# Masks of a 16-head attention: one half written to PSUM by ScalarE and one half added by TensorE products, changed to all written by ScalarE

## What is computed

```
score = jnp.einsum('bhqd,bhkd->bhqk', qh, kh) / jnp.sqrt(jnp.float32(DEPTH))
score = score + mask * jnp.float32(-1000000000.0)
attn = jax.nn.softmax(score, axis=-1)
out = jnp.einsum('bhqk,bhkd->bhqd', attn, vh)
```

```
logits = (logits + bias[None, None]) / jnp.sqrt(jnp.asarray(D, dt))
logits = jnp.where(mask, logits, jnp.finfo(dt).min)
```

## Time and profile before

| | us |
|---|---|
| median of 3 runs | 1736.21 |
| lowest and highest of them | 1733.26, 1736.88 |
| the profiled execution | 1738.16 |
| its span, from its first to its last instruction | 1736.3 |
| PE busy | 1259.2 |
| DVE busy | 1009.3 |
| ACT busy | 885.4 |
| POOL busy | 499.7 |

### The profile page before, as it was taken

The page is one execution under the profiler, slowest core; times in us unless marked ns, Lnnn a source line. Parts: engine busy times, 40 slices in busy tenths (PEclk is TensorE's granted clock), DMA queues, the critical chain, the costliest instruction groups (busy, mean ns, idle before and its releaser), DMA issues. The chain is left out here.

```text
span 1736.3 us, 21579 instructions
## 1 busy us (share of the span) xinstructions
PE 1259.2 (73%) x7168; PEld 628.1 (36%) x7168; DVE 1009.3 (58%) x2042; ACT 885.4 (51%) x1822; POOL 499.7 (29%) x583
## 2 busy tenths in 40 slices
PE   6998645266666749866537996973985979888896
PEld 2575421022222215522213553431433434543462
DVE  2573456999999536413833644442734748736852
ACT  2673234599999546743013772231652564743653
POOL 0362002388888531100302210000200213422440
PEclk9999866589999978978865997975887799989998
DMA  3000000000000034011023400014411500000000
GB/s 136 2 2 2 19 8 0 1 0 0 0 1 0 0 112 90 2 43 37 0 79 66 81 2 35 0 31 107 92 51 37 110 13 39 1 1 1 0 2 13
DMA packets 43486, 52.73 MB, mean 30 GB/s; under 512 B 2800, under 2 KB 39792, under 8 KB 41968
## 3 DMA queue, kind: packets, MB, share of 16 engines
q1 hardware_dynamic: 43376, 51.35, 11.4%
HBM read 36.66 MB, written 14.68 MB: 30 GB/s over the span
## 5 line engine op out<-in xcount | busy, mean ns | idle before, releaser
L1341 POOL TENSOR_TENSOR L_attn_z<-L_attn_state,L_attn_r 128x1024 f32<-128x1024 f32 x64 | 150.8, 2358 | 40.0 <-DVE L_attn_state L1327 33.5
L1327 DVE TENSOR_TENSOR_SCAN L_attn_state<-bank,L_attn_w 128x512 f32<-128x512 f32 x128 | 149.0, 1205 | 0.0
L1238 PE MATMUL bank<-L_attn_z,const 128*128 128x512 f32 x256 | 138.1, 667 | 1.4 <-POOL L_attn_z L1345 1.4
L791 DVE CUSTOM_DVE_ANT_0 L_xattn_core_logits<-bank,L_xattn_mask 128x256 f32<-128x256 f32 x256 | 98.6, 422 | 53.9 <-PE bank L574 41.4
L146 PE MATMUL bank<-x,weights 128*128 128x512 f32 (+1 forms) x108 | 60.0, 711 | 59.6 <-PEq L181 26.1
L1222 PE MATMUL bank<-L_attn_rows,L_attn_select 128*128 128x512 bf16 x96 | 36.9, 442 | 86.1 <-ACT L_attn_C L1290 43.2
L1278 ACT ACTIVATE L_attn_r<-L_attn_after_dt,L_attn_half_guard,L_attn_A 128x512 f32<-128x512 f32 x128 | 96.5, 802 | 0.0
L1268 ACT ACTIVATE bank<-L_attn_dt,L_attn_A 128x510 f32<-128x510 f32 x128 | 86.5, 676 | 13.3 <-DVE L_attn_state L1327 13.3
L703 ACT ACTIVATE L_xattn_core_probs<-bank 128x512 f32<-128x512 f32 x132 | 71.5, 596 | 36.9 <-PE bank L617 25.5
L574 PE MATMUL bank<-L_xattn_core_rows 48*128 48x256 bf16 x384 | 64.6, 312 | 32.2 <-DMA L_xattn_core_rows<-L_xattn_core_slots 18.0
L1345 POOL TENSOR_TENSOR L_attn_z<-L_attn_z,L_attn_C 128x1024 f32<-128x1024 f32 x32 | 75.7, 2367 | 23.7 <-ACT L_attn_C L1290 23.6
(11 more groups left out here) (466 smaller groups left out, 3029.9 us busy)
## 6 DMA issues: line engine op xcount, KB each, us to landing
L_xattn_core_rows<-L_xattn_core_slots SPq DMA_DIRECT2D x24, 384.0 KB, 5.8
weights<-in_pack_L_ffn SPq DMA_DIRECT2D x2, 2118.5 KB, 7.9
L_xattn_core_slots<-L_xattn_core_k_parts SPq DMA_DIRECT2D x24, 128.0 KB, 2.0
L_attn_core_rows<-L_attn_core_slots SPq DMA_DIRECT2D x8, 384.0 KB, 5.5
weights<-in_pack_L_ffn SPq DMA_DIRECT2D x1, 2824.0 KB, 9.4
weights<-in_pack_L_attn SPq DMA_DIRECT2D x1, 2304.0 KB, 8.5
L_xattn_core_slots<-L_xattn_core_q_parts SPq DMA_DIRECT2D x12, 192.0 KB, 2.2
weights<-in_pack_L_xattn SPq DMA_DIRECT2D x1, 1539.5 KB, 6.2
```

The lines of the kernel that those rows point to most:

```text
L791: last = nc.vector.tensor_tensor_reduce(logits[:, c], scores_bank[side][:, c * S:(c + 1) * S], mask[:, 2 * b + c, :], 1.0, MASKED, ALU.add ...
L1238: last = nc.tensor.matmul(y_bank[2 * c + half][:], ident, z[:, g % NS, c], start=False, stop=False, skip_group_check=True)
L1327: nc.vector.tensor_tensor_scan(state[:, g % NS, c, ::step], a_bank[c][:, ::step], w[:, g % 2, c, ::step], 0.0, ALU.mult, ALU.add).then_inc ...
L1341: nc.gpsimd.tensor_tensor(z[:, g % NS], state[:, g % NS], r[:, g % NS], ALU.mult).then_inc(z_done, 1)
```

## The change

The whole mask of both sides is now written by ACT, and everything that served the other way is gone:

- `preload(p)` writes two banks (two instructions) where it wrote one, and `shifted(p)` waits for both. No product of a masked stage starts a bank anew.
- the 6 products L617 of each step are gone, and `shifted_done` rises after each side's last L607 product, as it did in the stages without a mask.
- the making of `mask_parts` is gone: L680 and L683 on ACT, L744 and L748 on POOL, with their semaphores, their buffer and the two waits for `mask_split`.
- all four banks are marked as written at the start (4 products at L555 where there were 2).

```diff
@@ block.tensor
-                for at in (1, 3):
+                for at in range(4):
                     last = nc.tensor.matmul(shifted_bank[at][:], K.w("ident"), K.x[:, 0:HALF], start=True, stop=True)
...
                 if masked:
-                    pe.wait_ge(preloaded, p + 1)
+                    pe.wait_ge(preloaded, 2 * p + 2)
...
-                                         start=(not masked or c == 0) and not preloads(side), stop=False,
-                                         skip_group_check=True)
+                                         start=not masked, stop=False, skip_group_check=True)
                     for side in range(2):
-                        done = not masked or preloads(side)
                         last = nc.tensor.matmul(banks[side][:, c * S:(c + 1) * S], K.minus_rows[side_rows(side), t],
-                                                shifts[side_rows(side), n % 2, :], start=False, stop=done,
+                                                shifts[side_rows(side), n % 2, :], start=False, stop=True,
                                                 skip_group_check=True)
-                        if c == 1 and done and not masked:
+                        if c == 1:
                             last.then_inc(shifted_done, 1)
-                if masked:
-                    if p % SPB == 0:
-                        pe.wait_ge(mask_split, b + 1)
-                    for c in range(2):
-                        for part in range(3):
-                            last = nc.tensor.matmul(banks[0][:, c * S:(c + 1) * S], K.ident_bf,
-                                                    mask_parts[:, part, b, c * S:(c + 1) * S], start=False,
-                                                    stop=(part == 2), skip_group_check=True)
-                    last.then_inc(shifted_done, 2)
@@ block.scalar
             def preload(p):
                 n, t = divmod(p, 2)
-                nc.scalar.activation(shifted_bank[2 * t + 1][:], flat_mask(n // NG8), ACT.Copy).then_inc(preloaded, 1)
+                for side in range(2):
+                    nc.scalar.activation(shifted_bank[2 * t + side][:], flat_mask(n // NG8), ACT.Copy
+                                         ).then_inc(preloaded, 1)
 
             if masked:
-                for b in range(B):
-                    nc.scalar.activation(mask_parts[:, 0, b], flat_mask(b), ACT.Copy).then_inc(mask_rounded, 1)
-                for b in range(B):
-                    act.wait_ge(mask_less, b + 1)
-                    nc.scalar.activation(mask_parts[:, 1, b], mask_rest[:, b], ACT.Copy).then_inc(mask_rounded2, 1)
                 act.wait_ge(written, 1)
...
-                if masked and n == 1 and at == 0:
-                    act.wait_ge(mask_split, B)
@@ block.gpsimd
-            if masked:
-                for b in range(B):
-                    pool.wait_ge(mask_rounded, b + 1)
-                    nc.gpsimd.tensor_tensor(mask_rest[:, b], flat_mask(b), mask_parts[:, 0, b], ALU.subtract
-                                            ).then_inc(mask_less, 1)
-                for b in range(B):
-                    pool.wait_ge(mask_rounded2, b + 1)
-                    nc.gpsimd.tensor_tensor(mask_parts[:, 2, b], mask_rest[:, b], mask_parts[:, 1, b], ALU.subtract
-                                            ).then_inc(mask_split, 1)
```

## The result

| | before | after |
|---|---|---|
| median of 18 runs each, us | 1735.58 | 1738.63 |
| lowest and highest, us | 1733.26, 1736.88 | 1736.69, 1742.27 |
| profiled execution, and its span, us | 1738.16, 1736.3 | 1739.85, 1737.9 |

The ratio after to before is 1.0021, with a 95% interval of 1.0013 to 1.0028: 3 us slower by the medians, at the edge of what this kernel's measurement can tell from no change.

A forecast was written before the change was run, and what follows sets the result against it. PE's mask products bound the masked loops, then ACT would: +2.2 loop, -1.4 start, +0.5 allowance make +1.3 a stage, +2.6 for both, so 1736.2 + 2.6 = 1738.8 us; range 1733 to 1750.

The forecast's parts named there:

- the likeliest case: Whole kernel: measured within 0.2% of no change, 1732.7 to 1739.7 us, chance 0.53; slower 0.40, faster 0.07.
- The turn-over: Masked loops: ACT, with 12.8 us free, gets 15.0 and becomes the bound; loop 74.5 us, 2.2 longer.
- The second preload: ACT in the masked loop: one more 128x512 preload adds 0.50 us in each of 30 steps, 15.0 us.
- The start: Start of each masked loop: without the first six mask products the first exponential comes about 1.4 us earlier.
- The prelude: Before the masked loop: removing the sixteen ACT and POOL instructions that made mask_parts gains nothing, hidden behind DMA and scores.
- The allowance: Masked loops, near step 12 and at the start: ACT still waits 0.5 us a stage, bounds 0 and 2.
- rival 1: PE's clock falls in the masked loops: a third of steps lose 0.5 us, 10 us for both, 1749; chance 0.20.
- One sign of being wrong: Masked loops: the forecast is wrong if ACT's idle before exponentials remains over 5 us a stage.
- Rival 2: ACT's second preload costs 0.60, or engine waits add 0.1 a step: +6 for both stages, 1745; chance 0.15.
- Rival 3: Norm behind the attention: products L207 may get full clock, -3 us, with further gains 1732.5; chance 0.07.
- Rival 4: Masked loops: scores or values still hold PE, loop stays 72.3 us, -1.4 a stage at best, 1733.5; chance 0.03.

The follow-up runs named there:

- prelude_back: The changed kernel with the making of the unused mask_parts put back (8 instructions on ACT, 8 on POOL); 1740.26 us, ratio 1.0040.
- changed_again: The changed kernel run once more with the same code, for a second trace; 1738.85 us, ratio 1.0019.
- pe_only: The kernel before without the six mask products L617 a step, side 0 left unmasked, one preload a step as before; 1717.26 us, ratio 0.9905.
- act_only: The kernel before with a second ACT preload a step, PE waiting for both and the mask products L617 kept; 1743.6 us, ratio 1.0054.
- fill3: The changed kernel with three more PE products of zeros (128x256) in every step; 1742.67 us, ratio 1.0042.

## Why the prediction was right

**The time.** Forecast 1738.8, measured 1738.63; +2.6 against +3.0 by medians. That the two times agree within 0.2 us is luck in part, since the median of before was taken as 1736.21 and came out as 1735.58. A ratio within 0.2% was the likeliest case and slower the next, and 1.0021 lies on that bound.

**The turn-over** held. The sum of ACT's list was 74.5 us; the shortest loops of the changed kernel are 74.65 and 74.92 (prelude_back 74.75), and 74.3 to 74.4 without their disturbed steps. Steps of 2.15 and 2.41 us were forecast, 2.16 and 2.42 measured. The second preload was taken as 0.50; a pair now takes 1.06 until the next instruction (681.69 to 682.75) against 0.54 for one, so it is 0.52. An estimate of 0.52 is what the Trainium skill's figure gave (page "ScalarE: Activation LUTs", section "What ACT_TABLE_LOAD costs", 186 ns + 0.833 ns an element less 93 ns), and here it was nearer than the row of a pair alone. The 0.6 us that this adds was given back: two exponentials take 1.10 us until the preload and not 1.11 (0.3 in thirty steps), the logarithm and exponential of the sums 0.72 a time and not 0.82, and four exponentials in a row at the end 2.04 us and not 2.16.

**One reading was too simple.** The steady step of 2.18 is not the mean step of before. Over eight steps with `gathered` and the reciprocals the kernel before needs 19.52 us and the next eight 19.29, the changed one 19.51 to 19.53 where no step is disturbed: there they are nearly equal. The 2.3 us that the loop of changed_again lost are in the first ten steps (+1.2) and the last five (+0.6), where PE before had no `values` yet or no more scores to make, with 0.5 in between, most of it one disturbed step (3.19 us where its like take 2.88). The sum over the whole loop, on which the forecast went, contains this; the comparison of 2.28 with 2.18 does not.

**The start** was forecast 1.4 earlier and was 1.4 to 1.9 in four stages, 1.7 on average. The moment forecast for it, near 658.0, was missed because this execution reached the stage 1.5 us later. **The prelude** gave nothing back in the traces, as said: the first scores are under the DMA and the first exponential comes 17 us after ACT's preloads.

**The allowance** of 0.5 us a stage was half right in its reason and too small. It stood for `values` that ACT would wait for, near step 12 and at the start, with a block of `values` at the lower clock laid bare once as the upper bound. At the start this came true: the sixth exponential waits at a clock of 0.50, behind such a block, in three of the four loops of the changed kernel:

```profile
668.06 1.94 PE L615 MATMUL bank<-L_xattn_core_probs,v_heads 128*32 128x256 f32 x16
...
671.42 1.08 ACT L680 ACTIVATE L_xattn_core_rest<-bank 128x512 f32<-128x512 f32 x2 [0.32 <-PE bank L598]
```

That step came 0.4 to 0.6 us late. Later on, at full clock, no such wait is there (changed_again at 1010 to 1020 us); there ACT waited with the falls of the clock, which the forecast had only in rival 1. Together both cost 0.8, 3.1, 0.3 and 0.6 us in the four loops, 1.2 on average and over the bound of 2 in one. What this adds to the forecast, 0.7 a stage, is half made up by the start (0.3 more gained) and the loop without disturbances (0.1 less). So the mechanism was right and the sum is right within 0.3 us a stage, in part because the errors of its terms ran against each other.

One sign of being wrong did show in one place: ACT's idle before exponentials was to stay under 5 us a stage. It was 4.2 us in the first stage, and 5.8 in the second, of which 3.6 are before the first exponential and the rest is mostly the falls of the clock.

**Rival 1** happened as a mechanism and not as a price. The forecast listed a PEclk of 1.00 through most of the loop as its sign, and 0.79 to 0.85 was measured; by that sign it was wrong. The clock was 0.50 until 672.95 us where it had risen at 661.35 before, and it fell again three times. But a step was taken to decide above 2.28 us, with 2.36 for one at the lower clock. In the first steps, which have no `values`, exponentials were 2.16 and 2.42 apart at clock 0.50 too, with ACT busy 9.84 of 10: PE's list just fits. Only steps with `values` in double or with the sums came out longer. So the price of a third of the steps at 0.5 each, 10 us for both stages, was in fact 0.9 us (changed_again) to 3.9 (after) by the late steps of the traces, the sixth exponential included. The small idles between groups of products that come with it are the 0.40, 0.48 and 0.68 us shown above, after which the clock fell at 686.8 us; the Trainium skill (page "TensorE: Matmul & The Clock Gate", section "A second HAM failure mode: psum-queue depth-cycling") says that such idles can bring the clock up and down. The trace agrees with that in its order of events, though no run changed the idles by themselves, and not with the weight the rule would have had: the loop paid for few of its falls.

**Rival 2** is out: pairs take 1.12 us, under its sign of 1.15, and preloads 591 ns. **Rival 3**: the norm's four products L207 took 2.69 and 2.53 us in the first trace, 3.75 and 3.27 in the second, against 3.75 and 2.0. Together that is 0.5 less and 1.3 more for the same code, so the change doesn't decide it; the durations go with the clock that was granted at that moment. The rows, two of the first trace and one of the second:

```profile
740.13 2.69 PE L207 MATMUL bank<-L_xattn_outT,weights 128*128 128x512 f32 x4 [2.56 <-PEq L478]
...
1043.76 2.53 PE L207 MATMUL bank<-L_xattn_outT,weights 128*128 128x512 f32 x4 [2.56 <-PEq L478]
```

```profile
739.12 3.75 PE L207 MATMUL bank<-L_xattn_outT,weights 128*128 128x512 f32 x4 [2.56 <-PEq L478]
```

**Rival 4** is out: PE was released, as pe_only's loops of 64.8 and 65.2 us show.

## What to carry to other kernels

Where two engines work in turn, add up the whole list of the one that is to receive the work, over the whole loop, before anything else: here 12.8 us were free and 15.0 came, and this one comparison gave the loop within 0.2 us, the disturbed steps left out. When work leaves TensorE, look for where its clock will now be low, and there at the steps with the longest list; at the others, here, the time that PE has over hid the lower clock. What such steps cost changed from one execution to the next, 0.3 to 3.1 us a stage, so a range is all that a forecast can give for them. When neither engine is far from full, try to move part of the work: half of the steps gave 0.4% less than before where all of them gave 0.2% more. Try the shares on the chip, as the trace of one execution didn't rank them.

## What the runs showed that was not expected

- PE stayed at the lower clock with much to do: in after it was busy 9.43 of 10 us at 0.50 (660 to 670 us), mostly with products on 48 rows. In act_only, which has L617 on 128 rows in each step as before, the same stretch had 9.38 busy and a clock of 1.00:

```profile
660.00:670.00 10.00, 9.38 (x106) 5.51 (x103) 6.81 (x37) 9.87 (x21) 1.80 (x8) 1.00 0.58 103
```

Busy time alone therefore doesn't tell the granted clock. That the number of rows is what matters wasn't tried by itself: in fill3 with three 128-row products a step the clock was 0.50 there as well.

- Useless products can pay. Seventy-two products of zeros a stage, put where PE waited for ACT, made the changed kernel faster by about 0.25%, by ratios of different series of runs; with them in the first eight steps too it was some 0.2% slower.
